# Regrouping the expansions, the sums and the narrow projection in the last stage of a two-block convolution kernel

## The chip, the cores and the metric

The kernel runs on one core of one Trainium2 chip. The metric is the device time of one execution in microseconds; of three runs of the kernel before, the median was 664.91 (664.14 to 664.97). Everything is float32 except where the code says otherwise.

## What is computed

Two residual blocks on 32 images of 32 x 32 pixels and 64 channels: `x = x + L0(gn(x))`, then `x = x + L1(gn(x))`. `gn` is a group norm. L0 is a routed convolution in three steps; the change does not touch it. L1 is an involution, a convolution whose kernel is made from the pixel itself:

```python
r = jnp.einsum('bhwc,cd->bhwd', x, Wr) + br            # 64 -> 16 channels
r = jax.nn.relu((r - mean) * jax.lax.rsqrt(var + BN_EPS) * gamma + beta)
w = jnp.einsum('bhwd,dk->bhwk', r, Ws) + bs            # 16 -> 16 groups x 9 taps
xi = jnp.einsum('bhwc,cf->bhwf', x, Wi) + bi           # 64 -> 64 channels
...
out = jnp.sum(w * patches, axis=-1)                    # patches: 3 x 3 neighbours of xi
```

## The kernel before

Images are held in pairs: a tile of 128 partitions (two images of 64 channels) by 1024 pixels, 16 pairs in all. The program is written out by hand for each engine, with semaphores between them; nothing plans it at run time. The first six phases (L0) convolve; the last stage works through the 16 pairs one after the other, and the change is in that stage and in the two places of the last convolution (`beside`, L646) where its first projections are slipped in. A pair k goes through these steps, and TensorE's own order of them is the function `involve` at L833:

- `normalise2` (L1080, ScalarE) writes the normalised pair into one of two buffers `xn`.
- `project` (L624, TensorE), the narrow projection: 64 to 16 channels, two matmuls of 512 pixels into PSUM tile `att[:, 1]`, one for each half of the pixels. `empty_r` (L1094, ScalarE) applies batch norm and ReLU and rounds the result into `rstk`, the stack of 98 rows that the expansions read: high part, low part, high part again and two rows of ones. `r_lo` (L1789, GpSimd) writes the low part, `copy_high` (L476, a transfer on SyncE's queue) the second copy of the high part.
- `project_xi` (L632, TensorE), the wide projection, into the same PSUM tile; `empty_xi` (L1084, ScalarE) copies it with its bias into a padded image `xip`, in four operations on 64 partitions.
- `expand` (L803, TensorE): for each of nine taps, two matmuls of 512 pixels (its halves) turn the 98 rows into weights for 128 channels. They go into PSUM tile `conv`, which has two units of 1024 pixels; tap i uses unit i modulo 2, so tap i + 2 must wait until VectorE has read tap i.
- `product` (L1636, VectorE): two multiplications a tap (L1648), expansion times shifted `xip`, into a buffer of its own for each tap.
- `add_up` (L816, TensorE): the sums over taps, in five rounds of taps (0, 1), (2, 3), (4, 5), (6, 7), (8), as matmuls of 64 x 32 tiles into `att[:, 0]`. The profile counts two records for each float32 matmul, 16 for each call. `empty_sum` (L1105, ScalarE) copies the sums out, `finish` (L1797, GpSimd) adds the residual.
- `turn_back` (L795, TensorE): eight transpositions of the finished pair into `att[:, 1]`; `empty_pix` (L1114, ScalarE) copies them out and `store_pair` (L470, SyncE) writes them to memory.

`att[:, 1]` is thus used in turn by narrow projection, wide projection and transposition; the semaphores `misc_full` and `misc_free` count its uses, three a pair. TensorE's order for pair k is: expansions 0, 1; sums 3, 4 of pair k - 1; expansions 2, 3; narrow projection of pair k + 1; expansions 4, 5; sums 0; wide projection of k + 1; expansions 6, 7; sums 1, 2; expansion 8; transposition of k - 1. ScalarE's order (L1121) is: normalise k + 1, empty the sums of k - 1, empty the narrow projection, empty the wide one, empty the transposition. GpSimd alternates `finish(k - 1)` and `r_lo(k + 1)`; SyncE alternates `copy_high` and `store_pair`.

## Time and profile before

| what | value |
|---|---|
| median of three runs | 664.91 us |
| the profiled execution itself | 664.74 us |
| its span, first to last instruction | 663.0 us |
| TensorE matmul busy | 628.3 us, 95% |
| VectorE busy | 521.5 us, 79% |
| ScalarE busy | 326.9 us, 49% |
| GpSimd busy | 180.9 us, 27% |
| longest groups of the last stage | products L1648 177.9 us, expansions L813 95.7, sums L829 80.6 |

The profiled execution is one run under the hardware profiler; its rows are times within its span. PE is TensorE's matmuls, PEld its weight loads, DVE VectorE, ACT ScalarE, POOL GpSimd, SP SyncE. A matmul's record is longer than the time until the next one can start, since matmuls are pipelined, so the starts tell more than the durations.

### The profile page before, as it was taken

How to read it: one execution, taken by the hardware profiler on the slowest of the kernel's cores; microseconds unless marked ns; L12 is line 12 of the kernel's file. 1: busy time of each engine (PE TensorE's matmuls, PEld its weight loads, DVE VectorE, ACT ScalarE, POOL GpSimd, SP SyncE). 2: the span in 40 equal slices, each digit the busy share in tenths (PEclk: the TensorE clock that was granted, in tenths of full speed). 3: DMA queues.
4: the chain of work that ended last, by engine and by line, in shares of the span. 5: the costliest groups of instructions: out<-in, count | busy, mean ns of one | idle time of the engine just before them, and what ended most of it. 6: DMA issues, size and time to landing. Idle time of an engine off the chain costs nothing. (4 is left out here: it accounts for less than half of the span.)

```text
span 663.0 us, 15413 instructions
## 1 busy us (share of the span) xinstructions
PE 628.3 (95%) x5984; PEld 250.4 (38%) x5984; DVE 521.5 (79%) x816; ACT 326.9 (49%) x451; POOL 180.9 (27%) x193
## 2 busy tenths in 40 slices
PE   6869899899999999999999999989999999999995
PEld 6433333333333333333333323323444444444442
DVE  5689875998666776667687899949988888898885
ACT  3645532311432142224213656744787787787761
POOL 2100240006400720081018003512352243244230
PEclk9879999999999999999999999997999999999998
DMA  8930030032323243225312633000121312222132
GB/s 318 226 72 1 1 86 1 1 91 78 97 72 97 73 103 91 71 72 141 99 29 70 165 93 92 1 9 8 41 50 41 72 42 48 60 54 48 44 69 64
DMA packets 67461, 47.95 MB, mean 72 GB/s; under 512 B 53602, under 2 KB 54596, under 8 KB 67396
## 3 DMA queue, kind: packets, MB, share of 16 engines
q1 hardware_dynamic: 67108, 46.82, 28.5%
q8 instruction: 47, 0.77, 0.5%
q10 hardware_dynamic: 288, 0.21, 0.1%
q14 instruction: 18, 0.15, 0.1%
HBM read 35.15 MB, written 9.76 MB: 68 GB/s over the span
## 5 line engine op out<-in xcount | busy, mean ns | idle before, releaser
L758 PE MATMUL conv<-xpad,comb 64*64 64x512 f32 x2016 | 227.4, 596 | 4.4 <-DVE x L1385 4.2
L1648 DVE TENSOR_TENSOR x<-conv,x 128x512 f32<-128x512 f32 x288 | 177.9, 682 | 24.4 <-PE conv L813 23.1
L758 PEld LDWEIGHTS conv<-xpad,comb 64*64 64x64 f32 x2016 | 75.0, 134 | 136.6 <-issue 121.5
L813 PE MATMUL conv<-rstack,wse 98*128 98x512 f32 x288 | 95.7, 438 | 1.7 <-DVE xin L1431 0.9
L829 PE MATMUL att<-x,cmp 64*32 64x512 f32 x1280 | 80.6, 602 | 0.0
L813 PEld LDWEIGHTS conv<-rstack,wse 98*128 98x128 f32 x288 | 48.5, 190 | 70.7 <-DVE x L1648 64.0
L1317 DVE SCALAR_TENSOR_TENSOR xpad<-att,x 128x1024 f32<-128x1024 f32 x46 | 54.1, 1219 | 23.6 <-PE att L608 23.3
L959 ACT ACTIVATE x<-conv,bias 128x512 f32<-128x512 f32 x40 | 25.3, 683 | 90.9 <-PE conv L758 90.8
L1800 POOL TENSOR_TENSOR x<-x,xin 128x1024 f32<-128x1024 f32 x15 | 36.0, 2397 | 111.6 <-ACT x L1111 111.6
L950 ACT ACTIVATE comb<-experts,small 128x768 f32<-128x768 f32 (+1 forms) x33 | 27.4, 859 | 75.6 <-PE conv L727 45.4
L1727 POOL TENSOR_TENSOR rt<-rt 128x16 f32<-128x16 f32 x12 | 5.1, 423 | 196.5 <-ACT rt L922 195.8
L727 PE MATMUL conv<-row_sums,comb 64*64 64x512 f32 x480 | 55.4, 591 | 2.5 <-DVE row_sums L1353 1.3
L727 PE MATMUL conv<-xpad,comb 64*64 64x512 f32 x480 | 56.3, 597 | 1.1 <-ACT x L971 1.1
L1089 ACT ACTIVATE x<-att,small 64x512 f32<-64x512 f32 x64 | 44.0, 688 | 9.6 <-PE att L641 9.0
L1793 POOL TENSOR_TENSOR rstack<-x,rstack 32x1024 fp32r<-32x1024 f32 x16 | 38.2, 2385 | 23.3 <-ACT rstack L1103 23.3
L1111 ACT ACTIVATE x<-att 64x512 f32<-64x512 f32 x60 | 35.6, 593 | 15.1 <-PE att L829 14.0
L1422 DVE SCALAR_TENSOR_TENSOR comb<-experts,small,comb 128x768 f32<-128x768 f32 (+1 forms) x36 | 33.2, 950 | 2.9 <-ACT comb L950 2.8
L727 PEld LDWEIGHTS conv<-row_sums,comb 64*64 64x64 f32 x480 | 17.6, 132 | 35.6 <-issue 32.1
L727 PEld LDWEIGHTS conv<-xpad,comb 64*64 64x64 f32 x480 | 18.2, 131 | 33.7 <-issue 33.0
L829 PEld LDWEIGHTS att<-x,cmp 64*32 64x32 f32 x1280 | 18.6, 106 | 32.8 <-issue 30.2
L1118 ACT ACTIVATE comb<-att 128x1024 f32<-128x1024 f32 x15 | 15.4, 1027 | 31.1 <-PE att L800 31.1
L1099 ACT ACTIVATE x<-att,rsc 64x512 f32<-64x512 f32 x32 | 24.8, 775 | 10.0 <-PE att L629 9.5
(212 smaller groups left out, 755.9 us busy)
## 6 DMA issues: line engine op xcount, KB each, us to landing
experts<-forms SPq DMA_DIRECT2D x72, 192.0 KB, 3.9
experts<-forms SPq DMA_DIRECT2D x72, 144.0 KB, 2.9
x<-in_x SPq DMA_DIRECT2D x32, 256.0 KB, 5.5
out<-comb SPq DMA_DIRECT2D x30, 256.0 KB, 3.3
rstack<-rstack SPq DMA_DIRECT2D x16, 128.0 KB, 2.3
experts<-in_We SPq DMA_DIRECT2D x1, 1152.0 KB
forms<-experts SPq DMA_DIRECT2D x2, 576.0 KB, 5.7
out<-comb SPq DMA_DIRECT2D x4, 128.0 KB, 2.2
```

Of the source, the lines that this page charges most:

```text
L727: last = nc.tensor.matmul(conv[own[to], h, HW * rows:HW * rows + HW], comb[own[rows], q % 2, n, form * ROW + kw * C:form * ROW + kw * C + ...
L758: last = nc.tensor.matmul(conv[own[to], h, HW * rows:HW * rows + HW], comb[own[rows], q % 2, n, tap(t)], xpad[own[rows], 2 * (q % 2) + n, ...
L813: nc.tensor.matmul(conv[:, unit, cols], wse[:, ORDER[i], :], rstk[s][0:RR, cols], start=True, stop=True).then_inc(exp_full, 1)
L829: last = nc.tensor.matmul(att[q, 0, bank], sum_sel[own_rows, t + upper, :], prod[i][own_rows, cols], start=(r == 0), stop=(r == len(ROUNDS ...
L950: nc.scalar.activation(comb[:, q % 2, n, cols], first, ACT.Identity, scale=weight).then_inc(comb_begun[n], 1)
L1089: done = nc.scalar.activation(xip[s][own[n], 1 + 16 * h:17 + 16 * h, 1:W + 1], att[rows, 1, bank].rearrange("p (a b) -> p a b", b=W), ACT. ...
L1111: nc.scalar.activation(fin[64 * n:64 * n + 64, cols], att[rows, 0, bank], ACT.Copy)\
L1317: v.scalar_tensor_tensor(inner(q, n), img(att[:, use.unit, :]), 1.0, img(x[:, slot(q, n), :]), ALU.add, ALU.mult).then_inc(att_free[use.un ...
L1422: v.scalar_tensor_tensor(comb[:, q % 2, n, cols], chosen[:, n, 1, cols], weight(n, 1), comb[:, q % 2, n, cols], ALU.mult, ALU.add).then_in ...
L1648: v.tensor_tensor(img(prod[i])[:, rows, :], img(conv[:, unit, :])[:, rows, :], xip[s][:, kh + 16 * h:kh + 16 * h + 16, kw:kw + W], ALU.mul ...
L1793: v.tensor_tensor(rstk[s][32:64, :], r64[32:64, :], rstk[s][32:64, :].bitcast(F32), ALU.subtract)\
L1800: v.tensor_tensor(fin, fin, xin[:, k, :], ALU.add).then_inc(fin_ready, 1)
```

## The change

TensorE takes the expansions in groups of three between blocks of sums, with the wide projection ahead of the first sums and the transposition between expansions 7 and 8. The narrow projection is done for two pairs at once, in every odd pair behind expansion 1: four matmuls with 32 output columns each fill the 128 partitions of half a PSUM tile. ScalarE empties it with one operation on 128 partitions and rounds it with a second, GpSimd subtracts once for both pairs, and the rows of `rstk` are then filled by six transfers of 32 rows by 512 pixels for each pair. `att[:, 1]` is used five times in two pairs. The bank of a sum or of the wide projection follows the half of the pixels instead of the image, so that ScalarE's copies of one half join into one operation on 128 partitions: three copies instead of four for the sums and for the wide projection. Normalising runs three pairs ahead. The first projections move to later taps of the last convolution.

```diff
-PARTS_OF_SUM = 4
+PARTS_OF_SUM = 3
...
-        prod = [flat[:, n * S:(n + 1) * S] for n in (0, 1, 2, 3, 4, 5, 13, 14, 15)]
-        xn = [flat[:, (6 + n) * S:(7 + n) * S] for n in range(2)]
-        r64 = flat[0:TWO, 8 * S:9 * S]
+        prod = [flat[:, n * S:(n + 1) * S] for n in (0, 1, 2, 3, 4, 7, 13, 14, 15)]
+        xn = [flat[:, n * S:(n + 1) * S] for n in (6, 5)]
+        r_lo4 = flat[:, 8 * S:8 * S + HW]
+        r_hi4 = flat[:, 8 * S + HW:9 * S]
...
-            return slice(first, first + 64), slice(n * HW, (n + 1) * HW)
+            return slice(first, first + 64), slice(h * HW, (h + 1) * HW)
...
-            def copy_high(k, s):
-                eng.wait_ge(rhi_ready, k + 1)
-                eng.dma_start(rstk[s][TWO:AR, :].bitcast(F32), rstk[s][0:TWO // 2, :].bitcast(F32)).then_inc(rhi_copied[s], 16)
-
-            copy_high(0, 0)
-            copy_high(1, 1)
+            def fill(k, s, made):
+
+                eng.wait_ge(rhi_ready, made)
+                if not (isinstance(k, int) and k < 2):
+                    eng.wait_ge(exp_full, 2 * TAPS * (k - 1))
+                for first, part in ((0, r_hi4), (2 * ONE, r_hi4), (ONE, r_lo4)):
+                    if first == ONE:
+                        eng.wait_ge(rlo_ready, made)
+                    for h, cols in halves():
+                        rows = slice(2 * ONE * s + ONE * h, 2 * ONE * s + ONE * h + ONE)
+                        eng.dma_start(rstk[s][first:first + ONE, cols].bitcast(F32), part[rows, :]).then_inc(rstk_filled[s], 16)
+
+            for n in range(2):
+                fill(n, n, 1)
             with eng.Fori(0, GP - 1) as i:
                 for n in range(2):
-                    copy_high(2 * i + n + 2, n)
-                    store_pair(2 * i + n, n, 6 * i + 3 * n + 8)
-            store_pair(NP - 2, 0, 3 * NP)
+                    fill(2 * i + n + 2, n, i + 2)
+                    store_pair(2 * i + n, n, 5 * i + 2 * n + 7)
...
-            def project(k, s, m):
+            def project_two(k, m):
                 if not (isinstance(m, int) and m == 0):
                     eng.wait_ge(misc_free, m)
-                eng.wait_ge(xn_ready, k + 1)
-                for h, cols in halves():
-                    last = nc.tensor.matmul(att[own[h], 1, cols], wr[:, :], xn[s][:, cols], start=True, stop=True)
+                eng.wait_ge(xn_ready, k + 2)
+                for s in range(2):
+                    for h, cols in halves():
+                        first = 2 * ONE * s + ONE * h
+                        last = nc.tensor.matmul(att[first:first + ONE, 1, 0:HW], wr[:, :], xn[s][:, cols], start=True, stop=True)
...
-                    elif at == (3, 0, 6):
+                    elif at == (3, 1, 0):
                         eng.wait_ge(att_free[1], sum(u == 1 for u, _ in ATT_USES))
-                        project(0, 0, 0)
-                    elif at == (3, 1, 2):
+                        project_two(0, 0)
+                    elif at == (3, 1, 3):
...
-                    eng.wait_ge(rstk_ready, k + 1)
-                    eng.wait_ge(rhi_copied[s], 8 * (k - s) + 16)
+                    eng.wait_ge(rstk_filled[s], FILLS // 2 * (k - s) + FILLS)
...
+            def involve(k, s, m, first=False, last=False):
+
                 expand(k, s, 0)
                 if first:
                     eng.wait_ge(final_emptied, FINAL_PARTS)
                 expand(k, s, 1)
+                if s and not last:
+                    project_two(k + 1, m)
+                expand(k, s, 2)
                 if not first:
                     add_up(k - 1, 3)
                     add_up(k - 1, 4)
-                expand(k, s, 2)
-                expand(k, s, 3)
+                for i in (3, 4, 5):
+                    expand(k, s, i)
                 if not last:
-                    project(k + 1, 1 - s, m)
-                expand(k, s, 4)
-                expand(k, s, 5)
+                    project_xi(k + 1, 1 - s, m + s)
                 add_up(k, 0)
-                if not last:
-                    project_xi(k + 1, 1 - s, m + 1)
                 expand(k, s, 6)
                 expand(k, s, 7)
+                if not first:
+                    turn_back(k - 1, m if last else m + s + 1)
+                expand(k, s, 8)
                 add_up(k, 1)
                 add_up(k, 2)
-                expand(k, s, 8)
-                if not first:
-                    turn_back(k - 1, m if last else m + 2)
...
             def empty_xi(s, m):
                 eng.wait_ge(misc_full, m + 1)
+                nc.scalar.activation(xip[s][:, 1:17, 1:W + 1], img(att[:, 1, :])[:, 0:16, :], ACT.Identity, bias=bi_s[:, 0:1])
                 for n in range(2):
-                    for h in range(2):
-                        rows, bank = sum_of(n, h)
-                        done = nc.scalar.activation(
-                            xip[s][own[n], 1 + 16 * h:17 + 16 * h, 1:W + 1],
-                            att[rows, 1, bank].rearrange("p (a b) -> p a b", b=W), ACT.Identity, bias=bi_s[rows, 0:1])
+                    rows, bank = sum_of(n, 1)
+                    done = nc.scalar.activation(
+                        xip[s][own[n], 17:33, 1:W + 1],
+                        att[rows, 1, bank].rearrange("p (a b) -> p a b", b=W), ACT.Identity, bias=bi_s[rows, 0:1])
                 done.then_inc(misc_free, 1)
-            def empty_r(k, s, m):
+            def empty_two(made, m):
                 eng.wait_ge(misc_full, m + 1)
-                if not (isinstance(k, int) and k == 0):
-                    eng.wait_ge(rstk_ready, k)
-                for h, cols in halves():
-                    done = nc.scalar.activation(r64[:, cols], att[own[h], 1, cols], ACT.Relu, bias=rsc[own[h], 3:4],
-                                                scale=rsc[own[h], 1:2])
-                done.then_inc(misc_free, 1)
+                if not (isinstance(made, int) and made == 0):
+                    for s in range(2):
+                        eng.wait_ge(rstk_filled[s], FILLS * made)
+                nc.scalar.activation(r_lo4, att[:, 1, 0:HW], ACT.Relu, bias=rsc[:, 3:4], scale=rsc[:, 1:2]).then_inc(misc_free, 1)
                 eng.wait_ge(misc_free, m + 1)
-                nc.scalar.activation(rstk[s][0:TWO, :], r64, ACT.Copy).then_inc(rhi_ready, 1)
+                nc.scalar.activation(r_hi4.bitcast(F32R), r_lo4, ACT.Copy).then_inc(rhi_ready, 1)
             def empty_sum(k):
                 eng.wait_ge(sum_done, len(ROUNDS) * (k + 1))
+                nc.scalar.activation(fin[:, 0:HW], att[:, 0, 0:HW], ACT.Copy).then_inc(sum_emptied, 1)
                 for n in range(2):
-                    for h, cols in halves():
-                        rows, bank = sum_of(n, h)
-                        nc.scalar.activation(fin[64 * n:64 * n + 64, cols], att[rows, 0, bank], ACT.Copy)\
-                            .then_inc(sum_emptied, 1)
+                    rows, bank = sum_of(n, 1)
+                    nc.scalar.activation(fin[own[n], HW:S], att[rows, 0, bank], ACT.Copy).then_inc(sum_emptied, 1)
...
+            def involve(k, s, m, made=0, last=False):
+                if s and not last:
+                    empty_two(made, m)
+                if not (isinstance(k, int) and k == 0):
                     empty_sum(k - 1)
                 if not last:
-                    empty_r(k + 1, 1 - s, m)
-                    empty_xi(1 - s, m + 1)
-                if not first:
-                    empty_pix(k - 1, 1 - s, m if last else m + 2)
+                    empty_xi(1 - s, m + s)
+                if not (isinstance(k, int) and k >= NP - 3):
+                    normalise2(k + 3, 1 - s)
+                if not (isinstance(k, int) and k == 0):
+                    empty_pix(k - 1, 1 - s, m if last else m + s + 1)
             normalise2(0, 0)
-            empty_r(0, 0, 0)
+            normalise2(1, 1)
+            empty_two(0, 0)
             empty_xi(0, 1)
+            normalise2(2, 0)
...
-            def r_lo(k, s):
-                if isinstance(k, int) and k == 0:
+            def split_two(made):
+                if isinstance(made, int) and made == 1:
                     eng.wait_ge(nmr_ready, 5)
-                eng.wait_ge(rhi_ready, k + 1)
-                v.tensor_tensor(rstk[s][32:64, :], r64[32:64, :], rstk[s][32:64, :].bitcast(F32), ALU.subtract)\
-                    .then_inc(rstk_ready, 1)
-                eng.wait_ge(rstk_ready, k + 1)
+                eng.wait_ge(rhi_ready, made)
+                v.tensor_tensor(r_lo4.bitcast(F32R), r_lo4, r_hi4, ALU.subtract).then_inc(rlo_ready, 1)
+                eng.wait_ge(rlo_ready, made)
...
             with eng.Fori(0, GP - 1) as i:
-                involve(2 * i + 1, 1)
-                involve(2 * i + 2, 0)
-            involve(NP - 1, 1, last=True)
+                split_two(i + 2)
+                finish(2 * i)
+                finish(2 * i + 1)
+            finish(NP - 2)
```

The rest of the diff renames semaphores, changes the counts that are waited for, and takes the doubled columns out of `wr`.

## Rows read from the trace of the kernel before

**Rows 1.** Busy time by stage; PEclk: granted share of full clock.

```profile
core 0: us, PE busy (x) PEld busy (x) DVE busy (x) ACT busy (x) POOL busy (x), PEclk, DMA share, GB/s
...
444.50:459.80 15.30, 14.23 (x93) 5.28 (x89) 14.28 (x25) 6.08 (x8) 2.37 (x1) 0.78 0.04 9
...
473.90:639.70 165.80, 165.80 (x1639) 72.62 (x1639) 144.66 (x235) 128.58 (x169) 62.19 (x26) 1.00 0.23 53
...
447.60:455.00 7.40, 7.30 (x27) 2.35 (x35) 7.26 (x14) 2.61 (x3) 0.80 (x1) 0.55 0.00 0
```

**Rows 2.** The chain of waits from 473.9 to 639.7 us, shares by line.

```profile
by line: PE conv L813 40.9%; PE att L829 37.4%; PE att L629 7.9%; PE att L800 7.0%; PE att L641 6.7%
```

**Rows 3.** Groups of instructions, 473.9 to 639.7 us: busy us, mean ns | idle before.

```profile
L1648 DVE TENSOR_TENSOR x<-conv,x 128x512 f32<-128x512 f32 x235 | 145.4, 682 | 21.1 <-PE conv L813 20.2
...
L1800 POOL TENSOR_TENSOR x<-x,xin 128x1024 f32<-128x1024 f32 x13 | 31.2, 2397 | 101.7 <-ACT x L1111 101.7
...
L1111 ACT ACTIVATE x<-att 64x512 f32<-64x512 f32 x52 | 30.8, 593 | 10.0 <-PE att L829 9.0
```

**Rows 4.** Timeline 600 to 622 us, all engines: start, us, what.

```profile
604.71 4.87 DVE L1648 TENSOR_TENSOR x<-conv,x 128x512 f32<-128x512 f32 x8 [0.51 <-PE conv L813]
...
607.25 0.19 PEld L813 LDWEIGHTS conv<-rstack,wse 98*128 98x128 f32 x1 [0.41 <-DVE x L1648]
...
609.52 0.59 SPq L478 DMA_DIRECT2D rstack<-rstack  x1
...
609.75 2.79 ACT L1089 ACTIVATE x<-att,small 64x512 f32<-64x512 f32 x4 [0.25 <-PE att L641]
```

**Rows 5.** Who waited for whom, 473.9 to 639.7 us: total, times, longest.

```profile
DVE x L1648 <- PE conv L813: 20.2, 39, 0.5
```

**Rows 6.** Timeline of TensorE's matmuls alone, one pair.

```profile
604.17 1.20 PE L813 MATMUL conv<-rstack,wse 98*128 98x512 f32 x4
605.30 1.08 PE L629 MATMUL att<-x,wr 128*64 128x512 f32 x4
606.31 1.44 PE L813 MATMUL conv<-rstack,wse 98*128 98x512 f32 x4
607.68 1.09 PE L829 MATMUL att<-x,cmp 64*32 64x512 f32 x16
608.56 1.06 PE L641 MATMUL att<-x,wi 64*32 64x512 f32 x16
609.56 1.20 PE L813 MATMUL conv<-rstack,wse 98*128 98x512 f32 x4
610.69 1.95 PE L829 MATMUL att<-x,cmp 64*32 64x512 f32 x32
612.57 0.74 PE L813 MATMUL conv<-rstack,wse 98*128 98x512 f32 x2
613.14 1.06 PE L800 MATMUL att<-ident,x 128*128 128x128 f32 x8
613.96 1.17 PE L813 MATMUL conv<-rstack,wse 98*128 98x512 f32 x4
```

**Rows 7.** That timeline cut at 604.8 and 605.05 us.

```profile
604.51 0.86 PE L813 MATMUL conv<-rstack,wse 98*128 98x512 f32 x3
...
604.75 0.62 PE L813 MATMUL conv<-rstack,wse 98*128 98x512 f32 x2
```

**Rows 8.** Transfers issued from 473.9 to 639.7 us: KB each, median us to landing.

```profile
out<-comb SPq DMA_DIRECT2D x26, 256.0 KB, 3.3
rstack<-rstack SPq DMA_DIRECT2D x13, 128.0 KB, 2.3
```

**Rows 9.** Timeline of all engines shortly before the last stage.

```profile
431.36 1.24 ACT L1081 ACTIVATE x<-xin,nmr,rstd 128x1024 f32<-128x1024 f32 x1 [3.32 <-POOL nmr L1692]
...
432.75 1.08 PE L629 MATMUL att<-x,wr 128*64 128x512 f32 x4 [0.90 <-ACT x L1081]
```

More of the change, by code:

```diff
@@ L39 @@
 RR = 98
-TWO = 64
+ONE = 32
+FILLS = 16 * 6
+MISC_USES = 40
 T = S // 128
@@ L295, in build @@
         rhi_ready = sem("rhi_ready")
[L296 to L297 removed]
+        rlo_ready = sem("rlo_ready")
+        rstk_filled = [sem("rstk_filled0"), sem("rstk_filled1")]
         exp_full = sem("exp_full")
@@ L401, in build @@
         BLOCKS = [(wi[64 * n:64 * n + 64, 64 * n:64 * n + 64], A["Wi"]) for n in range(2)]
-        BLOCKS += [(wr[64 * n:64 * n + 64, 32 * a + CR * n:32 * a + CR * n + CR], A["Wr"])
-                   for n in range(2) for a in range(2)]
+        BLOCKS += [(wr[64 * n:64 * n + 64, CR * n:CR * n + CR], A["Wr"])
+                   for n in range(2)]
         CONSTS_IN = 16 * (len(CONSTS) + len(BLOCKS))
@@ L831, in add_up @@
                 last.then_inc(sum_done, 1)
-            def involve(k, s, first=False, last=False):
-                m = 2 if first else 3 * k + 2
+            def involve(k, s, m, first=False, last=False):
                 expand(k, s, 0)
@@ L868, in _ @@
             for k in range(1, NP):
-                involve(k, k % 2, last=(k == NP - 1))
+                involve(k, k % 2, misc_before(k), last=(k == NP - 1))
             add_up(NP - 1, 3)
             add_up(NP - 1, 4)
-            eng.wait_ge(misc_free, 3 * NP)
+            eng.wait_ge(misc_free, MISC_USES)
             eng.wait_ge(last_added, 4)
@@ L1119, in empty_pix @@
                     .then_inc(misc_free, 1)
-            def involve(k, s, first=False, last=False):
-                m = 2 if first else 3 * k + 2
-                if not last:
-                    normalise2(k + 1, 1 - s)
-                if not first:
+            def involve(k, s, m, made=0, last=False):
+                if s and not last:
+                    empty_two(made, m)
+                if not (isinstance(k, int) and k == 0):
                     empty_sum(k - 1)
                 if not last:
-                    empty_r(k + 1, 1 - s, m)
-                    empty_xi(1 - s, m + 1)
-                if not first:
-                    empty_pix(k - 1, 1 - s, m if last else m + 2)
+                    empty_xi(1 - s, m + s)
[3 more added lines that the diff above has]
+                    empty_pix(k - 1, 1 - s, m if last else m + s + 1)
             normalise2(0, 0)
-            empty_r(0, 0, 0)
+            normalise2(1, 1)
+            empty_two(0, 0)
             empty_xi(0, 1)
+            normalise2(2, 0)
             eng.wait_ge(residual_added, residuals(QUADS))
-            involve(0, 0, first=True)
-            involve(1, 1)
-            involve(2, 0)
+            involve(0, 0, 2)
+            for k in (1, 2, 3, 4):
+                involve(k, k % 2, misc_before(k), k // 2 + 1)
             eng.wait_ge(nmr_ready, 6)
-            with eng.Fori(1, GP - 1) as i:
-                involve(2 * i + 1, 1)
-                involve(2 * i + 2, 0)
-            involve(NP - 1, 1, last=True)
+            with eng.Fori(2, GP - 2) as i:
+                involve(2 * i + 1, 1, 5 * i + 4, i + 1)
+                involve(2 * i + 2, 0, 5 * i + 7)
+            for k in (NP - 3, NP - 2, NP - 1):
+                involve(k, k % 2, misc_before(k), k // 2 + 1, last=(k == NP - 1))
             eng.wait_ge(sum_done, len(ROUNDS) * NP)
@@ L1634, in _, with product @@
             eng.wait_ge(final_emptied, FINAL_PARTS)
-            def product(k, s, i, first):
+            def product(k, s, i, xi_emptied, first):
                 e = k * TAPS + i
@@ L1641, in product @@
                 if i == 0:
-                    eng.wait_ge(misc_free, 2 if first else 3 * k + 1)
+                    eng.wait_ge(misc_free, xi_emptied)
                 if not first:
@@ L1801, in finish @@
                 eng.wait_ge(fin_ready, k + 1)
-            def involve(k, s, first=False, last=False):
-                if not first:
-                    finish(k - 1)
-                if not last:
-                    r_lo(k + 1, 1 - s)
             eng.wait_ge(late_lo, 2)
-            r_lo(0, 0)
-            involve(0, 0, first=True)
+            split_two(1)
             inverse_root(5, slice(GP, NP), GP)
+            eng.wait_ge(nmr_ready, 6)
             with eng.Fori(0, GP - 1) as i:
-                involve(2 * i + 1, 1)
-                involve(2 * i + 2, 0)
-            involve(NP - 1, 1, last=True)
+                split_two(i + 2)
+                finish(2 * i)
+                finish(2 * i + 1)
+            finish(NP - 2)
 def constants():
```

27 lines of the change are left out of this document (14 added, 13 removed).

## The prediction

> **What bounds the kernel now.** I read the windows by stage first, then the chain of waits inside the last stage, then TensorE's order of work over one pair, then who waits for whom. The change touches only the last stage, whose even part lies between 473.9 and 639.7 us: 13 pairs of images in 165.80 us, 12.75 us a pair [rows 1]. There TensorE is busy for all of the window, VectorE for 144.66 us, ScalarE for 128.58, GpSimd for 62.19 [rows 1], and the chain of waits is TensorE from end to end: expansions (L813) 40.9%, sums (L829) 37.4%, narrow projection (L629) 7.9% [rows 2]. So TensorE sets the pace, but VectorE is close behind: a product of half an image takes 0.68 us alone [rows 3], eight in a row take 4.87 [rows 4], so one follows another by (4.87 - 0.68) / 7 = 0.60, and a pair's 18 make 10.77 us. The rest of its 12.75 is waiting: 39 waits of 0.52, three a pair [rows 5]. The reason is PSUM. It has two units for expansions, so at most four halves lie ahead of VectorE (2.4 us), and a block of sums lasts longer.
>
> TensorE's order, from the starts of its blocks [rows 6], written as "from its first start to the next block's start": four halves of expansions 1.13, projection 1.01, four halves 1.37, first sums with the wide projection 1.88, four halves 1.13, sums 1.88, two halves 0.57, transposition 0.82, and so on. Inside a run of four, the second half starts 0.34 after the first, the third 0.24 after that [rows 6, 7]; so two halves before sums cost 0.67 and two more 0.46. The 1.37 is a run in which the last half had to wait for VectorE: its weights are loaded at 607.25, 0.06 after the fourth product of the run from 604.71 ended (604.71 + 3 x 0.60 + 0.68 = 607.19), and the sums came 0.43 later [rows 4, 6].
>
> **Part by part: the groups of three.** Time t runs from the first half of expansion 0. In the trace the first product after a block of sums starts 0.54 after the first expansion (604.17 to 604.71) [rows 4, 6]. Expansion 2 overwrites the unit of expansion 0, so its halves wait for the products of 0, which end at 0.54 + 0.68 = 1.22 and 1.82; with 0.06 they start at 1.28 and 1.88, where they could have started at about 1.0 and 1.26. The sums follow 0.43 later, at 2.31. So a group of three costs 2.31, not 1.13 + 0.46 = 1.59, and the 0.72 of waiting outweighs what one run less is worth, 0.67 - 0.46 = 0.21.
>
> An **even pair**, then: sums of the pair before at 2.31, expansions 3 to 5 at 4.19, wide projection at 4.19 + 2.31 = 6.50, with the first sums behind it 1.88 as before, expansions 6 and 7 at 8.38. Four halves up to the transposition take 0.57 + 0.46 = 1.03, so it could start at 9.41. It now stands between expansions 7 and 8, and it needs the wide projection emptied by ScalarE. That emptying starts 1.19 after the projection (608.56 to 609.75) [rows 4, 6] and took 2.79 for four operations [rows 4]; the change makes three of it, 2.09. So it ends at 6.50 + 1.19 + 2.09 = 9.78, and the transposition starts at 9.84: a **new wait of 0.43**. Before, it came after expansion 8, and two more blocks hid the emptying. Expansion 8 is queued behind it: 9.84 + 0.82 = 10.66, then 0.67, sums 1.88, and the next pair begins at 13.21.
>
> An **odd pair** has the projection of two pairs behind expansion 1: 1.13 + 1.01 = 2.14 for expansion 2 (its wait is over by then), sums at 2.81, expansion 3 at 4.69, wide projection at 7.00, expansion 6 at 8.88, transposition 9.91 or, after ScalarE, 10.34, expansion 8 at 11.16, sums at 11.83, the next pair at 13.71. Against 12.75 that is 0.46 more in an even pair and 0.96 in an odd one. Seen from VectorE, its waits grow from 2.0 us a pair to 2.4 and 2.9, most of it before expansion 0, because the transposition and its wait now lie in front of the last product's expansion.
>
> **Prices the trace does not show.** The projection of two pairs is four matmuls of 32 columns side by side. Nearest rows: two of 64 columns, 1.01, and sixteen records of 32 columns in two rounds, 0.88 from 607.68 to 608.56 [rows 6]. I take 1.01; the ends are 0.5 (one round) and 2.0 (four rounds), -0.5 to +1.0 in six odd pairs, -3 to +6. Three emptyings on ScalarE at 0.70: the copy of the same size took 0.59 [rows 3], so the low end is 1.78 and the wait 0.12, -4; the high end is the old 2.79, +0.7 a pair, +9. Merged copies of sums cover 128 partitions instead of 64 with as many elements each; I cost them as one old one.
>
> **Banks of the sums.** The change also turns the assignment of PSUM banks: a sum's bank now follows the half of the image instead of the image, so the upper and the lower 64 input rows write into one bank at once, on other partitions of it. No row of the old trace has that; its blocks keep each half of the rows to a bank. With nothing changed the rounds stay at 0.43 (0.88 for two, 607.68 to 608.56 [rows 6]); at the other end they run one after the other. I take no change, since nothing in the rows shows TensorE holding back a matmul for a bank. The Trainium skill says (PSUM — Partial Sum Buffer, "PSUM bank collisions raise a hardware error") that different row tiles cannot access one bank at the same time, and also that the hardware neither arbitrates nor stalls; what that would make of these blocks is rival E.
>
> **What stays covered.** GpSimd's split of the low part now runs once for two pairs, ahead of the addition of the residual in its queue; the addition (2.40 [rows 3]) can start at 4.19 + 0.17 + three copies of 0.6 + 0.2 = 6.4 and ends at 8.8, 0.6 before the transposition could start. If that cover went, each 0.1 would delay expansion 8 by as much. ScalarE's normalising and two narrow emptyings fall into its idle time (128.58 busy of 165.80 [rows 1], and less work after). On SyncE six fills take the place of one copy, each issued in about 0.59 [rows 4] plus waits, 3.9 us a pair; the stores queue behind them, and a store's buffer is wanted only two pairs later. A fill for an even pair can start when the high part is rounded. The old copy was issued at 609.52, 4.2 after the projection's start at 605.30 [rows 4, 6], so at 1.13 + 4.2 = 5.3 of the odd pair at the latest; issued by 9.3 and landed 2.3 later [rows 8], at 11.6, before 13.71. It is hidden, with 2 us to spare; an odd pair's fill has a whole pair.
>
> **Where it starts and ends.** The first narrow projection waited 0.90 for ScalarE's normalising [rows 9]. It moves three taps later, where both its pairs are normalised (1.24 each [rows 9]): -0.9. Pairs 0 and 1 carry one-off statistics on VectorE (14.28 busy of 15.30 [rows 1]), so a part of pair 1's 0.96 is hidden there, while in pair 0 a block of sums (1.88) now lies ahead of the group norm's matmul and a projection (1.01) goes: I take +1.0 for both, between 0 and +2. The last pair has no projection either way: 0.
>
> **The sum.** Pairs 2 to 14 are seven even and six odd: 7 x 0.46 + 6 x 0.96 = 9.0. The profiled execution took 664.74 us (span 663.0, 1.7 around it), 0.17 under the median of 664.91. 664.74 + 9.0 + 1.0 - 0.9 = **673.8 us**, 1.3% slower.
>
> **Rivals.**
> **(A)** The transposition finds ScalarE done, since the emptying is quicker or its start earlier. Without the 0.43 the pairs take 12.78 and 13.28: 7 x 0.03 + 6 x 0.53 = 3.4, so 668.2. The margin is small against 2.09, which speaks for it; the row of 2.79 for four is steady, which speaks against.
> **(B)** Not slower: VectorE alone becomes the bound, each block of sums costs it 0.60 as now, and projection, transposition and waits of expansions vanish behind its work. Place: expansion 8 and the sums in front of expansion 0. A pair is then 10.77 + 3 x 0.60 = 12.57, 13 x 0.18 = 2.3 less, and 664.74 - 2.3 - 0.9 = 661.5. It decides when VectorE waits under 2.0 us a pair. For it speaks that TensorE's own work does fall, by a projection in two pairs; against it that four halves of cover do not reach over sums that start after a transposition.
> **(C)** The fills come late. The old single transfer landed 2.3 us after its issue [rows 8]; if the six ran one after the other, 5.3 + 13.8 = 19.1, 5.4 past 13.71, in seven pairs: 711. Stores issued in pairs on this queue do not show it: 26 with a median of 3.3 [rows 8]. The Trainium skill (SBUF — State Buffer, "The DMA setup-cost knee") gives every transfer a fixed 2 us and advises large ones; the old copy's 2.3 us for 128 KB agrees, and by it an estimate of 2.15 for 64 KB makes 12.9 for six in line, 4.5 us late each time, near 705. No row here shows six small ones in flight.
> **(D)** TensorE's clock falls in the waits. It was granted 0.55 of full speed, so mostly its 1.2 GHz level, from 447.6 to 455, when expansions came singly at VectorE's pace [rows 1]. If each pair had such a stretch of 7 us, half of it lost: 13 x 3.5 = 45, 719. In the new order only two halves of a group wait, and sums run at once behind them.
>
> **(E)** Halves of the rows that share a bank take turns. A pair has twelve rounds of sums and wide projection; doubled, 12 x 0.43 = 5.2 us more in each of 15 pairs: 673.8 + 77 = 751.
>
> **How the numbers follow.** Forecast 0.68, A 0.12, B 0.10, C 0.03, D 0.02, E 0.05. The range 665.5 to 678.5 holds A and the forecast with the likelier ends of its prices; B to E, 0.20, are left out. 0.2% is 1.3 us, about what a measurement of this kernel can tell from no change. B is faster, 0.10, with 0.01 of A; 0.03 of A falls within 0.2%; the rest is slower: 0.11, 0.03, 0.86.
>
> **What would show it.** In the new profile: pairs alternating between about 13.2 and 13.7 us; the third expansion of a group waiting for VectorE; a wait of about 0.4 before each transposition, ended by ScalarE; VectorE's longest waits, about 1.2, before expansion 0; the projection of two pairs as one block of about 1 us; no wait for a fill. The forecast is wrong if the period is under 12.75, if expansions 2 and 5 start without a wait, or if a fill or the clock shows in the chain.

## The result and the profile after

The changed kernel takes 675.61 us (median; 675.61 to 675.77) beside 664.75 for the kernel before in the same comparison: a ratio of 1.0166, 95% interval 1.0146 to 1.0186. A fourth run, left out of these numbers, took 1042.2 us at a mean granted clock of 0.557 where the other three had 0.98 (with it the median is 675.69), and no run shows why. The changed kernel is slower, by 1.8 us more than the 673.8 forecast and inside the range. The profiled execution took 675.61 us with a span of 673.8.

In the new listing the lines have moved: expansions are L829 (before L813), sums L845 (L829), the wide projection L658 (L641), the projection of two pairs L646 (L629), the transposition L817 (L800), VectorE's products L1663 (L1648), ScalarE's emptying of the wide projection L1101 and L1104 (L1089).

The period of a pair, from the first expansion of one pair to that of the next, is read from TensorE's timeline in every profile:

| kernel | first expansion | pair 0 | pair 1 | even, from 2 | odd, from 3 | first expansion of pair 15 | span |
|---|---|---|---|---|---|---|---|
| before | 444.54 | 15.23 | 13.88 | 12.77 | 12.73 to 12.77 | 639.46 | 663.0 |
| changed | 443.59 | 17.09 | 14.17 | 13.26 to 13.28 | 13.75 to 13.77 | 650.29 | 673.8 |

The 10.87 us between the two profiled executions divide so: the last stage starts 0.95 earlier; pairs 0 and 1 take 31.26 instead of 29.11, +2.15; pairs 2 to 14 take 175.44 instead of 165.81, +9.63; what follows pair 15's first expansion is the same within 0.1.

Busy time by stage after the change (columns as in [rows 1]): the first pair, the 13 pairs 2 to 14, and the stretch in which the clock is low.

```profile
443.60:460.70 17.10, 14.70 (x89) 5.50 (x85) 15.28 (x26) 3.31 (x4) 0.00 (x0) 0.70 0.06 16
474.85:650.29 175.44, 168.26 (x1643) 70.95 (x1635) 143.55 (x234) 85.43 (x114) 38.72 (x19) 1.00 0.29 69
446.00:453.00 7.00, 5.57 (x16) 2.24 (x24) 6.86 (x13) 0.00 (x0) 0.00 (x0) 0.55 0.00 0
```

Beside [rows 1], ScalarE's work in the pairs fell from 128.58 to 85.43 us and GpSimd's from 62.19 to 38.72. That was saved, but for about 2.5 us of ScalarE's 43 (two normalisings that now run ahead of these pairs), and it bought nothing. TensorE was busy for all of its window before and now idles 7.18 us of it; VectorE's idle time rose from 165.80 - 144.66 = 21.1 to 31.9 us. No engine is the bound alone any more. The chain of waits over the same pairs says so, where before it was TensorE from end to end [rows 2] (the line stands as printed, cut off at its end):

```profile
by line: PE att L845 28.0%; PE conv L829 20.3%; issue 10.3%; ACT x L1104 10.3%; PE att L817 8.6%; DVE x L1663 8.5%; PE att L658 8.2%; PE att L646 3.4%; DVEq L1662 1.1%; ACT x L1101 0.8%; DVEq L1659 0.3%; ACTq L1096 0.2%; ACTq L1127 0.2%; AC
```

ScalarE's L1104 is new on it. Who waited for whom in those pairs (total, times, longest):

```profile
DVE x L1663 <- PE conv L829: 31.9, 39, 1.2
...
PEld att L817 <- ACT x L1104: 9.1, 13, 0.7
```

VectorE still waits three times a pair, but up to 1.2 us instead of 0.5 [rows 5], and the transposition (L817) waits for ScalarE once in each of the 13 pairs. One even pair, TensorE's matmuls alone (columns as in [rows 6]):

```profile
609.97 2.37 PE L829 MATMUL conv<-rstack,wse 98*128 98x512 f32 x6
612.28 1.95 PE L845 MATMUL att<-x,cmp 64*32 64x512 f32 x32
614.15 2.39 PE L829 MATMUL conv<-rstack,wse 98*128 98x512 f32 x6
616.47 1.09 PE L658 MATMUL att<-x,wi 64*32 64x512 f32 x16
617.35 1.06 PE L845 MATMUL att<-x,cmp 64*32 64x512 f32 x16
618.35 1.19 PE L829 MATMUL conv<-rstack,wse 98*128 98x512 f32 x4
619.82 1.16 PE L817 MATMUL att<-ident,x 128*128 128x128 f32 x8 [0.28 <-ACT x L1104]
620.74 0.71 PE L829 MATMUL conv<-rstack,wse 98*128 98x512 f32 x2
621.38 1.95 PE L845 MATMUL att<-x,cmp 64*32 64x512 f32 x32
623.25 1.19 PE L829 MATMUL conv<-rstack,wse 98*128 98x512 f32 x4
624.38 1.06 PE L646 MATMUL att<-x,wr 128*32 128x512 f32 x8
625.37 0.74 PE L829 MATMUL conv<-rstack,wse 98*128 98x512 f32 x2
```

And from the timeline of all engines, the same pair as the other engines see it:

```profile
610.51 3.68 DVE L1663 TENSOR_TENSOR x<-conv,x 128x512 f32<-128x512 f32 x6 [1.21 <-PE conv L829]
...
611.25 0.19 PEld L829 LDWEIGHTS conv<-rstack,wse 98*128 98x128 f32 x1 [0.52 <-DVE x L1663]
611.85 0.19 PEld L829 LDWEIGHTS conv<-rstack,wse 98*128 98x128 f32 x1 [0.41 <-DVE x L1663]
...
614.69 3.68 DVE L1663 TENSOR_TENSOR x<-conv,x 128x512 f32<-128x512 f32 x6 [0.50 <-PE conv L829]
...
617.67 0.70 ACT L1101 ACTIVATE x<-att,small 128x512 f32<-128x512 f32 x1 [1.49 <-PE att L658]
...
618.38 1.39 ACT L1104 ACTIVATE x<-att,small 64x512 f32<-64x512 f32 x2
...
619.82 0.97 PEld L817 LDWEIGHTS att<-ident,x 128*128 128x128 f32 x8 [0.71 <-ACT x L1104]
```

The two waits of the forecast stand here. The fifth and sixth half of a group load their weights only when VectorE's products free the unit (waits of 0.52 and 0.41), so the group lasts 2.31. Behind the block of sums that follows VectorE waits 0.50, as it did behind such a block before [rows 5]. The transposition waits until ScalarE's third operation ends at 618.38 + 1.39 = 619.77 and starts at 619.82; expansion 8 is behind it, then the sums, and the next pair's first product has waited 1.23, as this pair's own had waited 1.21 (at 610.51).

### The profile page after: what moved, and what is told of

The parts are those of the page before. It is cut to its first block and busy times, and to the rows that moved or that the text cites. A ratio compares the mean times of both kernels' runs of the same rounds, so it can differ in the third digit from the quotient of the medians.

```text
span 673.8 us, 15376 instructions
## 1 busy us (share of the span) xinstructions
PE 628.1 (93%) x5984; PEld 247.9 (37%) x5984; DVE 520.3 (77%) x816; ACT 277.9 (41%) x388; POOL 152.5 (23%) x185
## 5 line engine op out<-in xcount | busy, mean ns | idle before, releaser
L1663 DVE TENSOR_TENSOR x<-conv,x 128x512 f32<-128x512 f32 x288 | 176.6, 683 | 36.8 <-PE conv L829 36.7
L829 PE MATMUL conv<-rstack,wse 98*128 98x512 f32 x288 | 102.3, 449 | 7.3 <-DVE x L1663 2.0
L845 PE MATMUL att<-x,cmp 64*32 64x512 f32 x1280 | 80.0, 600 | 0.0
L829 PEld LDWEIGHTS conv<-rstack,wse 98*128 98x128 f32 x288 | 49.7, 191 | 78.7 <-DVE x L1663 60.7
L845 PEld LDWEIGHTS att<-x,cmp 64*32 64x32 f32 x1280 | 20.7, 107 | 37.5 <-issue 26.2
L1121 ACT ACTIVATE x<-att 128x512 f32<-128x512 f32 x15 | 9.0, 601 | 52.3 <-PE att L845 52.3
L1451 DVE BATCH_NORM_STATS2 stats<-xin 128x6 f32<-128x512 f32 x40 | 27.3, 682 | 3.3 <-ACT xin L920 2.4
L1704 POOL TENSOR_TENSOR rstd<-variance,mhalf 128x4 f32<-128x4 f32 (+1 forms) x6 | 7.9, 1314 | 93.5 <-DVE variance L1191 93.4
L1384 DVE TENSOR_TENSOR xpad<-xpad 128x1088 f32<-128x1088 f32 x20 | 28.0, 1440 | 0.3
L1392 DVE TENSOR_TENSOR x<-x,conv 128x1024 f32<-128x1024 f32 x10 | 12.2, 1220 | 20.5 <-PE conv L744 20.5
```

Of the source, the lines that this page charges most:

```text
L829: nc.tensor.matmul(conv[:, unit, cols], wse[:, ORDER[i], :], rstk[s][0:RR, cols], start=True, stop=True).then_inc(exp_full, 1)
L845: last = nc.tensor.matmul(att[q, 0, bank], sum_sel[own_rows, t + upper, :], prod[i][own_rows, cols], start=(r == 0), stop=(r == len(ROUNDS ...
L1384: v.tensor_tensor(rows, rows, pads[:, :, first + 2:H + first + 1:2, :], ALU.subtract)\
L1451: gn.then(v.bn_stats(stats[:, k, n, :], xin[:, k, n * HW:(n + 1) * HW]))
L1663: v.tensor_tensor(img(prod[i])[:, rows, :], img(conv[:, unit, :])[:, rows, :], xip[s][:, kh + 16 * h:kh + 16 * h + 16, kw:kw + W], ALU.mul ...
```

## The experiments

All start from the changed kernel unless said otherwise. The theory: the new order puts more work between expansions than the four halves in PSUM cover, and lets the transposition meet ScalarE too early; the single edits (projection of two pairs, six fills, merged copies, banks) cost nothing themselves. A call of `add_up` or `project_xi` takes two rounds (0.88 in all); two of them in a row make a block of four rounds, 1.88 up to the next expansion. e1, e3 and e4 ran once each.

Periods of all seven. In e5 to e7 the projection of two pairs stands ahead of an odd pair's first expansion (in e7 not in pair 1) and is counted to the pair before it.

| run | pairs 0, 1 | even, odd | us | span |
|---|---|---|---|---|
| e1_short_empty | 16.98, 13.64 | 12.75, 13.23 | 668.02 | 666.2 |
| e2_old_order | 15.58, 13.92 | 12.75, 12.75 | 665.15 (median) | 663.9 |
| e3_turn_behind8 | 16.42, 14.36 | 13.46, 13.95 | 678.64 | 676.8 |
| e4_average_early | 16.68, 13.78 | 13.27, 13.76 | 674.85 | 673.1 |
| e5_two_round_blocks | 19.99, 13.00 | 12.78, 12.02 | 663.08 (median) | 661.9 |
| e6_first_pair_old | 19.04, 11.77 | 12.78, 12.02 | 661.50 (median) | 659.6 |
| e7_second_pair_late | 16.57, 13.27 | 12.78, 12.02 | 659.96 (median) | 658.9 |

### e1_short_empty: a shorter emptying

ScalarE's two operations on the lower half of the padded wide image (rows 17 to 32) are left out; the first one stays.

```diff
-                nc.scalar.activation(xip[s][:, 1:17, 1:W + 1], img(att[:, 1, :])[:, 0:16, :], ACT.Identity, bias=bi_s[:, 0:1])
-                for n in range(2):
...
+                done = nc.scalar.activation(xip[s][:, 1:17, 1:W + 1], img(att[:, 1, :])[:, 0:16, :], ACT.Identity, bias=bi_s[:, 0:1])
```

> ScalarE empties only the upper half of the wide projection (one operation of 0.69 us instead of three, 2.1); the lower half of the padded image stays zero. Theory (the transposition's wait for this emptying is one of three causes): the wait before the transposition goes, pairs take 12.8 and 13.3 us instead of 13.28 and 13.75, 14 x 0.48 = 6.7 less, about 669. Rival 1 (the wait is hidden behind VectorE's work, the groups of three cost everything): pairs unchanged, 675 to 676. Rival 2 (the wait is the whole loss): back to about 664.

668.02 us, 7.59 less than the changed kernel's 675.61. The waits over the 13 pairs no longer hold the transposition at all, and VectorE's are shorter:

```profile
DVE x L1658 <- PE conv L829: 25.2, 39, 1.0
```

Each pair is 0.52 shorter, even and odd alike: 13 x 0.52 = 6.8 of the 7.59, nearly all of the rest lies before them (0.64 in pairs 0 and 1). The wait itself is 0.42 of the 0.52: the transposition starts at 9.43 of an even pair (603.98 to 613.41) instead of 9.85. The rest is its own length, 0.80 to the next expansion instead of 0.92. The even pairs are back at 12.75, with their groups of three, so these cost an even pair nothing by themselves. The 0.48 that is left in the odd ones goes with the projection in front of expansion 2, which they alone have: behind the sums that follow it VectorE waits 1.00 (product at 621.95), in an even pair 0.52 (608.72).

### e2_old_order: all parts of the change, the old order

```diff
                 expand(k, s, 1)
-                if s and not last:
-                    project_two(k + 1, m)
-                expand(k, s, 2)
                 if not first:
                     add_up(k - 1, 3)
                     add_up(k - 1, 4)
-                for i in (3, 4, 5):
-                    expand(k, s, i)
+                expand(k, s, 2)
+                expand(k, s, 3)
+                if s and not last:
+                    project_two(k + 1, m)
+                expand(k, s, 4)
+                expand(k, s, 5)
+                add_up(k, 0)
                 if not last:
                     project_xi(k + 1, 1 - s, m + s)
-                add_up(k, 0)
                 expand(k, s, 6)
                 expand(k, s, 7)
-                if not first:
-                    turn_back(k - 1, m if last else m + s + 1)
-                expand(k, s, 8)
                 add_up(k, 1)
                 add_up(k, 2)
+                expand(k, s, 8)
+                if not first:
+                    turn_back(k - 1, m if last else m + s + 1)
...
-                split_two(i + 2)
                 finish(2 * i)
+                split_two(i + 2)
```

ScalarE empties a sum ahead of the narrow projection, as before.

> TensorE's old order of expansions, sums, wide projection and transposition; projection of two pairs, fills and merged copies stay; ScalarE and GpSimd empty the old sums before the narrow projection. Theory (VectorE's waits over three blocks of sums set the pace, not TensorE's work): dropping every second projection gains nothing, even and odd pairs take about 12.75 us each, total 663.5 to 665, the start 0.9 earlier. Rival (TensorE's work sets the pace): even pairs lose the projection, 11.7 to 11.8, odd 12.75, total about 657.

665.15 us, ratio 1.0004 (0.9995 to 1.0014) to the kernel before. The whole loss lies in the order. But nothing is gained either: an even pair now has no narrow projection and an odd one has it, and both take 12.72 to 12.78. Who waited for whom, from 486 to 640 us:

```profile
DVE x L1664 <- PE conv L829: 20.3, 36, 2.1
```

Three waits of about 0.5 a pair, as in [rows 5], behind each block of four rounds of sums. VectorE's 18 products and these three waits make the period; TensorE's saved microsecond becomes TensorE waiting. The 2.1 is one event: pair 14 took 14.34 instead of 12.75, and the granted clock of three stretches (columns as in [rows 1]) shows where.

```profile
629.15:632.80 3.65, 3.29 (x16) 1.42 (x8) 3.13 (x7) 1.79 (x3) 1.45 (x1) 0.95 0.79 188
632.80:636.10 3.30, 3.30 (x33) 0.66 (x32) 1.76 (x3) 0.00 (x0) 0.92 (x1) 0.54 0.25 62
603.60:607.10 3.50, 3.11 (x16) 1.42 (x8) 2.98 (x6) 1.78 (x3) 1.29 (x1) 1.00 0.85 200
```

An even pair's eight halves in a row came at VectorE's pace (from 629.15), and the sums and the wide projection behind them ran at 0.54, near the lower of its two levels (1.2 and 2.4 GHz). The same eight halves at 603.6 kept 1.00.

### e3_turn_behind8: the transposition behind expansion 8

```diff
                 expand(k, s, 7)
+                expand(k, s, 8)
                 if not first:
                     turn_back(k - 1, m if last else m + s + 1)
-                expand(k, s, 8)
                 add_up(k, 1)
```

> Only the transposition moves, from between expansions 7 and 8 to behind expansion 8, ahead of the sums. Theory: its wait for ScalarE goes, but expansion 8 then waits for product 6 and VectorE has nothing ahead of it while the transposition and four rounds of sums run: pairs of about 13.45 and 13.95, 678 to 679. Rival (the wait for ScalarE is what costs): 13.28 and 13.75 fall to 12.8 and 13.3, about 669.

678.64 us, 3.0 slower than the changed kernel. ScalarE is done when the transposition starts, and it costs more: the last group is a group of three, and transposition and sums stand together in front of the next product. The timeline at a pair's first product:

```profile
611.83 3.68 DVE L1663 TENSOR_TENSOR x<-conv,x 128x512 f32<-128x512 f32 x6 [1.41 <-PE conv L829]
```

So a wait taken away is not time won: what counts is how much TensorE does between two expansions. Here the transposition takes 0.99 and the sums 1.88 (608.43 to 611.30), and VectorE waits 1.41 behind them. A block of 1.88 costs it 0.50 (614.69 in the changed kernel), so the length that is free is about 1.4 us, an estimate from 1.88 - 0.50 and 2.87 - 1.41, and not the 2.4 of four halves. The rows of the changed kernel show why: when its block of sums starts, at 612.28, the products behind the group run on until 610.51 + 3.68 = 614.19, 1.91 more, and the next product starts only 0.54 after its own expansion (609.97 to 610.51).

### e4_average_early: the group norm's matmul ahead of the first pair's sums

```diff
                 expand(k, s, 8)
+                if first:
+                    average_late()
                 add_up(k, 1)
                 add_up(k, 2)
```

The function holds the three waits and the matmul that stood behind the first pair. The changed kernel's timeline in that place:

```profile
452.36 1.96 PE L658 MATMUL att<-x,wi 64*32 64x512 f32 x16
...
456.79 3.68 DVE L1663 TENSOR_TENSOR x<-conv,x 128x512 f32<-128x512 f32 x6 [1.29 <-PE conv L829]
...
458.55 1.95 PE L845 MATMUL att<-x,cmp 64*32 64x512 f32 x32
...
460.43 0.40 PE L881 MATMUL att<-mv,wide 128*128 128x16 f32 x2
...
460.86 0.17 DVE L1186 TENSOR_SCALAR negmean<-att 128x8 f32<-128x8 f32 x1 [0.40 <-PE att L881]
```

> In the first pair the matmul of the last group norm comes ahead of the last block of sums instead of behind it. Theory (VectorE waits there for this matmul): the second pair's first product starts 0.7 to 0.9 earlier, total about 674.8. Rival (the first pair is long only because TensorE runs at half its clock there): no change, 675.6.

674.85 us; pairs 0 and 1 take 30.46, 0.80 less than in the changed kernel, and VectorE's group norm no longer waits:

```profile
456.39 3.68 DVE L1668 TENSOR_TENSOR x<-conv,x 128x512 f32<-128x512 f32 x6 [0.99 <-PE conv L829]
...
458.08 0.29 PE L854 MATMUL att<-mv,wide 128*128 128x16 f32 x2
...
459.99 0.15 DVE L1191 TENSOR_SCALAR negmean<-att 128x8 f32<-128x8 f32 x1
```

Not all of the 0.80 is the matmul's. The products behind the first sums had already waited 0.99 instead of 1.29, ahead of the place of the edit: from 455.9 to 457.0 us the granted clock was 1.00 in this run and 0.55 in the changed kernel's. So about 0.3 goes with the clock, which the edit does not explain, and about 0.5 with the matmul behind the sums; that the total came out as expected is in part luck. The rest of the 2.15 that pairs 0 and 1 lost, some 1.6, was not taken apart. e2, with the old order, takes 29.50 there, 0.39 more than the kernel before, but at a granted clock of 0.69 from 446 to 457 us instead of 0.53, so order and clock are not told apart. A part that the rows show: the wide projection and the first sums last 0.88 + 1.00 = 1.88 at 616.47, but 3.59 at 452.36 (to the next expansion at 455.95), where the granted clock is near the lower level (0.50 from 450.0 to 455.9). In the kernel before, the same two took 2.75 (453.31 to 456.06).

### e5_two_round_blocks: shorter blocks between the expansions

If the theory holds, an order in which at most one block stands between two expansions should be faster than both kernels.

```diff
+                if s and not last:
+                    project_two(k + 1, m)
                 expand(k, s, 0)
...
+                beside_taps = {1 + s: sums_before, 3 + s: wide, 4 + s: lambda: add_up(k, 0), 6 + s: back, 7 + s: sums}
+                for i in range(1, TAPS):
+                    if i in beside_taps:
+                        beside_taps[i]()
                     expand(k, s, i)
```

The names stand for the same calls as before: the sums of the pair before, the wide projection, the transposition, sums 1 and 2. Wide projection and first sums are now two blocks of two rounds with an expansion between them, and the transposition stands by itself; the sums of the pair before and sums 1 and 2 stay blocks of four rounds.

> Only TensorE's order changes against the changed kernel: the wide projection and the first sums are blocks of two rounds with an expansion between them, the sums of the pair before come behind expansion 0 (odd pairs 1), the transposition behind expansion 5 (6), the last sums behind 6 (7), the projection of two pairs ahead of expansion 0 of odd pairs. Theory (VectorE has four halves, 2.4 us, of cover: a block of two rounds is covered, one of four costs it 0.6): VectorE waits less than 1.6 us a pair, two pairs take about 24.7 us (12.0 and 12.7), total about 660, faster than both kernels. Rival 1 (more runs cost TensorE more than VectorE gains): near 664. Rival 2 (each break costs VectorE the same whatever its length): five breaks a pair, 13.8, about 680.

663.08 us, ratio 0.9971 (0.9960 to 0.9983): faster than the kernel before. Two pairs take 24.80 instead of 25.5, close to what was expected, and the chain of waits from 476 to 637 us is TensorE again, with VectorE's waits down from 20.2 [rows 5] to 17.4 us:

```profile
by line: PE conv L829 42.0%; PE att L845 38.5%; PE att L658 8.2%; PE att L817 7.2%; PE att L646 3.7%; issue 0.3%; DVEq L1667 0.1%; DVE x L1668 0.0%; DVEq L1664 0.0%
```

The total was missed by 3 us, in pair 0, which took 19.99. There four rounds of sums ran at the low clock (0.50 from 454 to 458 us), 3.59 to the next expansion, and VectorE's products came late behind them:

```profile
455.00 3.66 PE L845 MATMUL att<-x,cmp 64*32 64x512 f32 x32
...
459.42 2.48 DVE L1668 TENSOR_TENSOR x<-conv,x 128x512 f32<-128x512 f32 x4 [2.81 <-PE conv L829]
```

Of the 19.99, 16.50 lies ahead of the group norm's matmul (460.01). The rest is the projection of two pairs: first in pair 1's queue, it waits 1.93 for VectorE's group norm and starts at 462.23, and expansion 0 follows at 463.51.

### e6_first_pair_old: e5 with the old order in the first pair

```diff
+                if first:
+                    for i in range(1, 6):
+                        expand(k, s, i)
+                    add_up(k, 0)
+                    project_xi(k + 1, 1 - s, m)
+                    expand(k, s, 6)
+                    expand(k, s, 7)
+                    add_up(k, 1)
+                    add_up(k, 2)
+                    expand(k, s, 8)
+                    return
```

> The order of blocks of two rounds as in the kernel before this one, but the first pair keeps the old kernel's order (expansions 0 to 5, first sums, wide projection, expansions 6 and 7, last sums, expansion 8). Theory (the first pair lost what the others gained, since sums of four rounds at half the clock stand in front of products that VectorE then waits for): first pair 15.6 us instead of 20.0, the others unchanged at 12.0 and 12.8, total 658.5 to 660. Rival (the first pair is long because of its statistics and the clock alone, whatever the order): 19 to 20 us, total 662 to 663.

661.50 us, ratio 0.9950 (0.9932 to 0.9967). Pairs 0 and 1 take 30.81 instead of 32.99: half of what was expected, and pair 0's 19.04 is where the rival had it. The theory of this run did not hold: up to the group norm's matmul (460.24) pair 0 takes 16.46, beside 16.50 in e5. e2, with the same order there, took 15.44, at a granted clock of 0.69 from 446 to 457 us instead of 0.55. What was gained lies behind that matmul: 0.9 up to pair 1's first expansion and 1.23 in pair 1, where the granted clock from 464 to 466 us was 0.50 in e5 and 1.00 here. One wait of e5 is still there, shorter: the projection of two pairs, first in pair 1's queue, needs the group norm, and the expansions stand behind it.

```profile
461.83 1.06 PE L646 MATMUL att<-x,wr 128*32 128x512 f32 x8 [1.29 <-DVE gnt L1203]
```

### e7_second_pair_late: e6 with that projection behind expansion 1 of pair 1

```diff
-                if s and not last:
+                if s and not last and k > 1:
                     project_two(k + 1, m)
...
+                    if k == 1 and i == 2:
+                        project_two(k + 1, m)
```

> As the kernel before this one, but in the second pair alone the projection of two pairs stands behind expansion 1 instead of ahead of expansion 0. Theory (the projection there waits 1.29 us for VectorE's group norm, with all of the second pair queued behind it): the first two pairs take 29.4 to 29.8 us instead of 30.8, total about 660.3. Rival (the half clock of TensorE alone makes them long): 30.8 as before, total 661.5.

659.96 us, ratio 0.9928 (0.9904 to 0.9953), the lowest median of all: 0.7% under the kernel before and 2.3% under the changed one's median. Its interval overlaps that of e6; the profile shows the step, for pairs 0 and 1 take 29.84 instead of 30.81, close to what was expected. Over the pairs from 476 to 637 us (columns as in [rows 1]) TensorE is busy for 160.60 of 161.00 us.

```profile
476.00:637.00 161.00, 160.60 (x1620) 69.03 (x1628) 143.39 (x234) 85.60 (x114) 38.97 (x19) 1.00 0.32 75
```

Beside the profiled execution of the kernel before, 4.07 less: -0.92 for the start, +0.73 in pairs 0 and 1, -4.98 in pairs 2 to 14 (160.83 instead of 165.81), and +1.08 after pair 15's first expansion (the sum is within 0.02).

## Why the prediction was right

**The groups of three**: right to the hundredth in size, 2.31 from 609.97 to 612.28, with the two waits for VectorE in the rows. That the shortage of PSUM units causes it rests on these waits; a third unit was not tried. The 0.72 is TensorE's waiting and not time lost by itself: VectorE's wait behind such a group and its sums is 0.50, the old one, and e1's even pairs take 12.75 with the groups in place.

**The new wait of the transposition**: right in place, cause and size. The transposition was put at 9.84 of an even pair and came at 9.85. Its wait was forecast at 0.43, and without it the transposition starts 0.42 earlier (e1). What was too small is the block itself: it takes 0.92 to the next expansion (619.82 to 620.74), not 0.82, and with expansion 8 taking 0.64 instead of 0.67 that is the 0.07 by which an even pair (13.28) exceeds the 13.21. VectorE's longest waits, put at about 1.2 before expansion 0, are 1.21 and 1.23 there.

**Even and odd pairs**: forecast +0.46 and +0.96, measured about +0.51 and +1.00. Over pairs 2 to 14 that makes 9.63 instead of 9.0.

**The prices that no row showed**: the projection of two pairs takes 0.99 (624.38 to 625.37), taken as 1.01; three emptyings take 0.70 + 1.39 = 2.09, as taken.

**The start**: -0.95, forecast -0.9. **The last pair**: 0 within 0.1.

**The term that was mis-sized**: pairs 0 and 1. They were put at +1.0 between 0 and +2 and took +2.15, outside these bounds. The prediction named the block of sums in front of the group norm's matmul, but set it off against the projection that goes; by e4 it costs about 0.5. And it priced the first pair's blocks at full clock although [rows 1] showed 0.55 there; the wide projection and the first sums alone took 3.59, where the kernel before had 2.75. The 1.15 too little here, 0.63 in the pairs, 0.05 too much at the start and 0.07 outside the span make nearly all of the 1.8 between 673.8 and 675.61.

**What was misread and did not reach the sum.** "TensorE sets the pace" does not hold: e2 projects once for two pairs in the old order, and the period stays 12.75 with VectorE's three waits of 0.5. So VectorE and these waits set the pace before, too; the sum came out because it followed VectorE's products through every group. The reason given for the waits, that a block of sums lasts longer than the 2.4 us of four halves, is not right either: the block lasts 1.88, and e3 puts the free length at about 1.4. And VectorE's waiting was put at 2.0 us a pair where [rows 5] has 3 x 0.52 = 1.6.

**The rivals.** A: the wait is there in all 13 pairs; e1 takes it away and lands at 668.02 where A stood at 668.2. B: VectorE alone was to set 12.57; even where the old order gives it three short waits (e2), the period is 12.75, and the saved projection gains nothing. Its price was too low by its own rows: with a block of sums at 0.60 "as now" it must give the 12.75 of now. The changed kernel never came near. C: no line of the waits names a fill. Of the pairs' transfers

```profile
rstack<-x SPq DMA_DIRECT2D x78, 64.0 KB, 2.0
```

78 landed a median of 2.0 us after their own issue, six issued in 3.76 us:

```profile
600.19 3.76 SPq L493 DMA_DIRECT2D rstack<-x  x6
```

The last of these was thus out by 603.95 and, at that median, landed by about 606, 4 us before 609.97. The fixed 2 us for each that the Trainium skill gives (SBUF — State Buffer, "The DMA setup-cost knee") agrees; what failed is the rival's assumption that the six would pay it one after the other. D: 1.00 was granted over the pairs. e2 shows that the risk was not empty: one stretch of 3.3 us at 0.54 cost 1.6 us there. E: blocks of four rounds take 1.87 (621.38 to 623.25) as before [rows 6], so halves that share a bank do not take turns. The Trainium skill (PSUM — Partial Sum Buffer, "PSUM bank collisions raise a hardware error") says that the hardware does not stall for a bank; the time agrees with that. The old assignment of banks alone was not tried.

## What to carry to other kernels

When one engine feeds another through a double buffer, count the cover, and read it from the feeding engine's blocks and the fed engine's waits: here four halves are 2.4 us of VectorE's work, but a block of 1.88 already costs 0.5 and one of 2.87 costs 1.4, so about 1.4 us is free and what lies beyond is paid. Shorter blocks lower these waits (e5), while a longer group of feeds only fills the buffer and makes the feeding engine wait. Before moving a step earlier, look up what used to hide the wait it now meets. Work taken off an engine buys time only once the order lets that engine be the bound: the halved projection was worth nothing in the old order (e2), while in e5's, where TensorE is the bound, two pairs take 24.80 instead of 25.5. How much of that is the projection was not run; a second projection at 0.99 would bring the two pairs to 25.8, an estimate.

## What was not expected of the hardware

Expansions that came one by one at VectorE's pace left TensorE busy for 5.57 of 7 us and yet at a granted 0.55, and the blocks behind them paid for it: 3.59 for a block of 1.88 in e5. When the full clock came back was not the same from run to run either: with one order in pair 0, the group norm's matmul came after 15.44 us in e2, 16.46 in e6 and 16.42 in e7. The same pattern inside the even part brought the clock down in one pair of e2 and not in another, so it is a risk and no fixed price. Six small transfers on one queue overlapped: the old copy of 128 KB landed in 2.3 [rows 8], each of the 64 KB fills in 2.0 with the next already issued.
